# Dynamic time warping stage of a decoder kernel: low weight halves by TensorE and ScalarE, a wider backward scan, one comparison inside the forward waves, paths read back batch by batch

## The chip, the core and the metric

The kernel runs on one core of a Trainium2 chip. The metric is the device time of one execution in microseconds (us). A core has a matrix engine (TensorE, in the profile PE, its weight loads PEld), a vector engine (VectorE, DVE), a scalar engine (ScalarE, ACT), a general engine (GpSimd, POOL) and a queue engine (SyncE, SP) that here issues all transfers (DMA). The engines run on their own and wait for each other on semaphores.

## The reference, cut to what matters

Two decoder layers on x of shape (4, 1024, 256). The change lies in two neighbouring parts of the second layer:

```python
x = x + _L1_xattn_ref(ctx_1024, _layernorm(x))      # alignment by dynamic time warping
x = x + _L1_ffn_ref(_layernorm(x), sim, gates, q_proj, k_proj, v_proj, o_proj)   # 16 experts

def _align_one(small, large):           # small: 77 context rows, large: 1024 rows
    D = _pairwise_euclidean(small, large)
    R = _dtw_cost(D)                    # R[i,j] = D[i,j] + min(R[i-1,j], R[i,j-1], R[i-1,j-1])
    i_idx, j_idx, valid = _backtrack(R, T_small, T_large)   # from the corner: diagonal, up or left
    return zeros.at[j_idx].add(small[i_idx] * valid)        # a column of the path takes its rows

def _gating(h, sim, gates):
    logits = _l2norm(h, -1) @ _l2norm(sim, 0) - sigmoid(gates)      # then top choices and softmax
```

## The kernel before, in words

Four batches pass one after the other through the first layer, the cosine attention and the distances to the context rows, which are written to a padded tensor in memory. Then `finish_*` (lines 2314 to 2346) does, for all four batches together, the warping and then the experts. Only this end is touched.

**Forward waves.** The 1024 columns are cut into 16 lanes of `LW` = 64 columns. A batch takes 32 partitions, of which 16 hold its lanes, so the four batches lie side by side. Lane l works on context row w - l in wave w, so there are `WAVES` = 92 waves. A wave on DVE (`wave`, lines 1334 to 1347) is a minimum of two shifted views of the row before (L1342), a shuffle that brings the neighbour lane's last cell (L1344), and a scan along the 64 columns (L1346). ACT copies each row from a ring of four (`rows4`) into `costs` (`keep`, L1279) and, between rows, squares the expert weights for their scale. The distances come in three pieces of waves (`PIECES`): POOL fills a piece with a large number, then SP loads it (lines 1231 to 1236). POOL also sets the seeds, and the first wave waits for `seeds_set`.

**Between.** Four passes over 92 x 64 cells (L1374 to L1380) make 0/1 masks in 16 bits: whether the path came from above (`came_up`), whether from the diagonal (`came_diag`), and `left`, which is 1 - `came_up`.

**Backward waves.** Turns 0 to 91 walk back from the last wave (`wave_back`, lines 1391 to 1407): an addition of what moved down from the previous turn into `inject` (L1401), a shuffle (L1402), a scan in reversed order, cell = left x cell + inject (L1404), and a product of the step masks with the new row (L1407), which gives the next turn's two addends in `taken`. The first turns are written out, the rest is a loop of 22 turns of four waves each. ACT copies each row into `path_cells` (L1310), which may lag by no more than the ring of four rows.

**Weights in two halves.** Between groups of four rows ACT prepares the expert weights: 32 parts of 128 x 384 and 8 of 128 x 512. It scales a part in place (L1491, L1484) and rounds it to 16 bits, the high half (L1496, L1487). POOL subtracts the high half from the scaled part and writes the low half (`split_low_pool`, L1502, L1508). The halves overwrite parts that are done, so a part waits for an earlier one. TensorE does nothing in this stage.

**From the path to the experts.** SP stores the path in three pieces, waits for all, and loads all four batches' rows with one transfer (L1248), then `sim` and `gates` (L1565, L1566). ACT squares `sim`, TensorE sums it, POOL takes a power (L1580), and DVE scales `sim` before it copies the path rows. Then TensorE multiplies path and context rows (`align_pe`, L1631), DVE adds and normalizes, TensorE transposes, ACT copies the transposed rows (L275), squares the eight row tiles for the norm (`square_z`, L1789), and makes the high half of the transposed rows (L1793). DVE makes the low half, then the gate's choices (some 25 short instructions), and the expert products start.

Every engine executes its own instruction list in the written order. There is no planner; the order is that of the functions `dtw_*`, `split_*` and `experts_*`.

Of the kernel before, what the change touches and what calls it, by code (L numbers as in the profile page):

```python
# [15 lines left out]
F16 = mybir.dt.float16  # L16
# [69 lines left out]
def program(nc, t, out):  # L86

    ctx = ExitStack()
    with ctx:
# [1117 lines left out]
        left = r.take(WAVES, LW + 2, dt=BF16)  # L1207
# [4 lines left out]
        taken = zr.take(2, 2, LW + 1)  # L1212
        inject = zr.take(LW)
        path_padded = nc.dram_tensor("path", (B, PADDED, T), F32)
        skew_loaded = [sem(f"skew_loaded_{i}") for i in range(3)]
        dtw_done, path_in = sem("dtw_done"), sem("path_in")
# [14 lines left out]
        def dtw_sp(sp):  # L1231
            sp.wait_ge(pad_stored, 16 * 2 * B)
            for i, (w0, w1) in enumerate(PIECES):
# [14 lines left out]
            sp.dma_start(path_rows, path_padded.ap()[:, PAD:PAD + S2, :].rearrange("b i j -> i b j")).then_inc(path_in, 16)  # L1248

        def dtw_pool(g):  # L1250
# [11 lines left out]

            step(g.memset(rows4, BIG))
            step(g.memset(taken, 0.0))
            for b in range(B):
# [5 lines left out]
                step(g.memset(taken[32 * b:32 * b + 1, 1, 0, LW - 1:LW], 1.0))  # L1271
# [3 lines left out]
        def dtw_act(a):  # L1275
# [27 lines left out]
            with a.Fori(end + O_SUMS, WAVES // 4) as i:  # L1303
                for k in range(4):
                    keep(4 * i + k, k)
            a.wait_ge(w_root, 2)

            def keep_path(turn, k):
                a.wait_ge(path_row_ready, turn + 1)
                a.activation(path_cells[:, turn * -1 + (WAVES - 1), :], rows4[:, k, 0:LW], ACT.Copy).then_inc(path_kept, 1)  # L1310
# [3 lines left out]
            split_part(a, 0, True)  # L1314
            split_part(a, 1, True)
# [5 lines left out]
            for i in range(DC * E // 2, WAVES // 4):  # L1321
                for k in range(4):
                    keep_path(4 * i + k, k)
                for m in ((0, 1) if i == DC * E // 2 else (i - DC * E // 2 + 1,)):
                    split_o(a, m)

        def dtw_dve(v):
            own = Own(v, dtw_own)
            own(v.memset(costs[:, 0, :], BIG))
            v.wait_ge(seeds_set, 2 + 2 * B)  # L1330
# [3 lines left out]
            def wave(w, k, first):  # L1334
# [10 lines left out]
                own.wait()  # L1345
# [7 lines left out]
            def waves(first_turn, end):  # L1353
                with v.Fori(first_turn, end) as i:
                    own.enter(i - first_turn, 8)
# [14 lines left out]
            diag, above, beside = costs[:, 0:WAVES, 0:LW], costs[:, 0:WAVES, 1:], costs[:, 1:, 0:LW]  # L1370
            came_up, came_diag = step[:, :, 0, 0:LW], step[:, :, 1, 0:LW]
# [1236 lines left out]
```

## Time and profile before

| | before |
|---|---|
| median of three runs | 3520.44 us (3519.69 to 3520.49) |
| profiled execution, its own time | 3520.67 us |
| its span | 3519.0 us |
| busy over the span | PE 2756.7, DVE 2473.3, ACT 1352.1, POOL 649.7 us |
| mean granted TensorE clock | 0.872 of full speed |

The span runs from the first to the last recorded instruction. The warping begins 2381 us into it and the experts fill the rest from about 2684 us. A row of a timeline gives start, duration, engine, line of the kernel, operation, output and inputs, and in brackets the idle time before it with what ended that time. Stage rows give for each engine its busy time and its number of instructions, then the granted TensorE clock (1.00 is full speed).

### The profile page before, as it was taken

The page shows a single profiled execution, that of the slowest core. Times are in us where ns is not written, and L with a number is a line of the kernel's source. Part 1 is how long each engine was busy: PE and PEld are TensorE (multiplying, and loading weights), DVE is VectorE, ACT ScalarE, POOL GpSimd, SP SyncE. Part 2 cuts the span into 40 slices and gives each one's busy share as a digit, 9 for nine tenths or more (in the row PEclk, how much of TensorE's full clock was granted, in tenths as well). Part 3 has the DMA queues.
Part 4 walks back from the last instruction along what each step waited for, and adds up shares of the span by engine and source line. Part 5 has one row for each costly group of instructions (what it writes and reads, how often), then busy time and mean ns, then how long its engine had stood idle before and what let it go on. Part 6 is the DMA issues. An engine that isn't in the chain of part 4 may idle for free.

```text
span 3519.0 us, 37233 instructions
## 1 busy us (share of the span) xinstructions
PE 2756.7 (78%) x12144; PEld 1595.1 (45%) x12144; DVE 2473.3 (70%) x4930; ACT 1352.1 (38%) x2514; POOL 649.7 (18%) x457
## 2 busy tenths in 40 slices
PE   3225989996988997889997989980006999999998
PEld 2003854443764434665344854440004656556564
DVE  6995587986487996487996585016875677676766
ACT  2323316753325763324772316544341141221313
POOL 2443001341000331100333000000121040130404
PEclk9557789998899998789998799995557999999999
DMA  4001000101000001000101000105010000000000
GB/s 151 0 0 43 1 1 10 25 16 47 1 1 7 22 19 50 1 1 1 25 19 53 1 1 10 28 13 116 0 16 17 1 1 13 1 13 1 13 1 13
DMA packets 57593, 65.85 MB, mean 19 GB/s; under 512 B 27723, under 2 KB 46656, under 8 KB 56768
## 3 DMA queue, kind: packets, MB, share of 16 engines
q1 hardware_dynamic: 57408, 63.51, 6.7%
q8 instruction: 101, 1.65, 0.2%
q14 instruction: 84, 0.69, 0.1%
HBM read 45.22 MB, written 9.88 MB: 16 GB/s over the span
## 4 chain that ended last, share of the span: by engine, by line
PE 56%; DVE 28%; issue 5%; ACT 2%; POOL 2%; DMA 2%; DVEq 1%; SPq 0%; POOLq 0%; ACTq 0%
PE psum L1667 13%; DVE arena L542 6%; PE psum L383 6%; PE psum L931 3%; PE psum L786 3%; PE psum L1727 3%; DVE arena L537 3%; PE psum L766 3%; PE psum L1045 3%; PE psum L949 2%; PE psum L1087 2%; PE psum L777 2%; PE psum L269 2%; PE psum L373 2%; PE psum L374 2%
## 5 line engine op out<-in xcount | busy, mean ns | idle before, releaser
L1667 PE MATMUL psum<-weights,arena 128*128 128x384 f16 x3072 | 534.7, 329 | 6.1 <-DVE arena L2028 3.2
L383 PE MATMUL psum<-arena,weights 128*128 128x512 f32 (+1 forms) x1024 | 523.0, 593 | 5.0 <-ACT arena L458 5.0
L458 ACT ACTIVATE arena<-psum,minus_scale 128x512 f32<-128x512 f32 x512 | 350.7, 686 | 216.8 <-PE psum L383 215.0
L2031 DVE SCALAR_TENSOR_TENSOR arena<-psum,arena 128x384 f32<-128x384 f32 x480 | 295.8, 616 | 193.1 <-PE psum L1667 182.0
L1667 PEld LDWEIGHTS psum<-weights,arena 128*128 128x128 f16 x3072 | 304.2, 99 | 195.0 <-issue 11.6
L597 POOL TENSOR_TENSOR arena<-arena 128x1024 f32<-128x1024 f32 x128 | 274.0, 2140 | 600.7 <-DVE arena L542 600.1
L542 DVE TENSOR_TENSOR_SCAN arena<-weights,arena 128x1026 f32<-128x1026 f32 x128 | 293.9, 2296 | 19.5 <-ACT weights L451 3.8
L246 POOL TENSOR_SCALAR shifted<-mean_var 128x4 f32<-128x4 f32 x40 | 10.0, 250 | 1216.6 <-DVE mean_var L223 1216.1
L1907 POOL TENSOR_TENSOR arena<-arena 128x512 f32<-128x512 f32 x112 | 147.7, 1322 | 405.7 <-ACT arena L1848 395.3
L383 PEld LDWEIGHTS psum<-arena,weights 128*128 128x128 f32 (+1 forms) x1024 | 166.1, 163 | 98.8 <-ACT arena L458 12.1
L451 ACT ACTIVATE weights<-arena,weights 128x512 f32<-128x512 f32 x256 | 169.1, 712 | 102.8 <-DVE arena L542 102.8
L373 PE MATMUL psum<-arena 128*128 128x512 f16 x512 | 194.3, 379 | 4.7 <-DMA arena<-arena 4.7
L374 PE MATMUL psum<-arena 128*128 128x512 f16 x512 | 194.0, 379 | 0.0
L275 ACT ACTIVATE z_both<-psum 128x512 f32<-128x512 f32 x96 | 55.9, 596 | 321.2 <-PE psum L269 320.9
L1727 PE MATMUL psum<-weights,arena 128*128 128x512 f16 x768 | 172.5, 379 | 7.8 <-DVE x_all L2060 4.6
L269 PE MATMUL psum<-ident,z_both 128*128 128x128 f32 x384 | 74.4, 354 | 122.0 <-DVE z_both L260 102.2
L931 PE MATMUL psum<-weights,z_both 128*128 128x352 f32 x512 | 164.6, 476 | 6.2 <-DVE arena L1000 3.4
L550 DVE TENSOR_TENSOR arena<-arena,psum 128x1024 f32<-128x1024 f32 x128 | 156.4, 1222 | 4.4
L537 DVE TENSOR_TENSOR arena<-arena,psum 128x1024 f32<-128x1024 f32 x128 | 154.8, 1210 | 4.6 <-PE psum L356 3.6
L2060 DVE SCALAR_TENSOR_TENSOR x_all<-psum,arena,x_all 128x256 f32<-128x256 f32 x256 | 122.3, 483 | 50.0 <-PE psum L1727 44.9
L1592 PE MATMUL psum<-arena,ones 128*128 128x16 f32 x4 | 1.0, 372 | 198.8 <-ACT arena L1585 198.8
L766 PE MATMUL psum<-arena 128*128 128x308 f32 x256 | 124.8, 660 | 21.3 <-DVE arena L879 18.2
(316 smaller groups left out, 4979.1 us busy)
## 6 DMA issues: line engine op xcount, KB each, us to landing
arena<-arena SPq DMA_DIRECT2D x64, 128.0 KB, 2.3
arena<-head_inv SPq DMA_DIRECT2D x32, 256.0 KB, 3.4
weights<-in_qkv SPq DMA_DIRECT2D x2, 3072.0 KB, 17.1
weights<-gate_upT_kept SPq DMA_DIRECT2D x4, 1408.0 KB, 6.1
x_all<-in_x SPq DMA_DIRECT2D x4, 1024.0 KB, 12.1
weights<-in_cWkv SPq DMA_DIRECT2D x4, 1024.0 KB, 10.7
out<-x_all SPq DMA_DIRECT2D x4, 1024.0 KB, 4.4
weights<-downT_kept SPq DMA_DIRECT2D x4, 640.0 KB, 7.1
```

What stands on the lines that cost most here:

```text
L373: pe.matmul(psum[:, i % 3, :], keys, q_parts[:, hd, at], start=True, stop=False)
L374: pe.matmul(psum[:, i % 3, :], keys, q_swapped_parts[:, hd % 2, at], start=False, stop=True).then_inc(s2_psum, 1)
L383: pe.matmul(psum[0:rows, 3 + turn % 2, :], value_and_ones(kt, hd), expd[:, i % 2, :], start=kt == 0, stop=kt == NT - 1).then_inc(pv2_done, 1)
L458: a.activation(expd[:, i % 2, :], psum[:, i % 3, :], ACT.Exp, bias=minus_scale[:, :], scale=SCALE / QK ** 2).then_inc(exp_done, 1)
L537: v.tensor_tensor(to[:, :, 1:], u[:, :, at], both(5 + 2 * j % 3), ALU.mult).then_inc(w_done, 1)
L542: v.tensor_tensor_scan(flat, dA[:, j % RING].rearrange("p m x -> p (m x)"), flat, 0.0, ALU.mult, ALU.add).then_inc(scan_done, 1)
L597: g.tensor_tensor(y[:, :, at], y[:, :, at], h[:, j % RING, :, 1:], ALU.add).then_inc(y_added, 1)
L766: last = pe.matmul(psum[:, 2 * m + i, 0:SH], qT[:, m, k * P:(k + 1) * P], k_heads[:, m, 4 * i:4 * i + 4, :].rearrange("p h s -> p (h s)"), ...
L931: last = pe.matmul(psum[:, 2 * i + half, 0:FQ], zT[:, c, k * P:(k + 1) * P], wT[:, c, half * FQ:(half + 1) * FQ], start=c == 0, stop=c == ...
L1667: last = pe.matmul(psum[:, n % PROJ_BANKS, 0:W3], zT_parts[:, of_z, c, k * P:(k + 1) * P], w_parts[:, c, e, of_w, :], start=c == 0 and j == 0,
L1727: last = pe.matmul(psum[:, O_BANKS[u % 4], :], ao_parts[:, of_a, k * P:(k + 1) * P], o_parts[:, m, of_w, :], start=j == 0, stop=j == 2)
L2031: step_ = v.scalar_tensor_tensor(qkv[:, k, :], src, router_w[:, k, e:e + 1], qkv[:, k, :], ALU.mult, ALU.add)
```

## The change

1. POOL's subtraction of the halves is gone. ACT writes the high half from the unscaled part with the scale folded in. TensorE forms (scale x identity) x part minus identity x high half in a PSUM bank, and ACT copies the bank to the low half.
2. A backward turn has no addition. Row and addends are interleaved: `taken` holds two addends per cell, `left_and_one` holds `left` and a constant one, so a scan of 128 elements does cell = left x cell + a, then cell = 1 x cell + b. The rows are now 2 x 64 wide, the product reads and writes every second element. POOL writes the ones before it sets the seeds.
3. The comparison for `came_diag` is made per forward wave between shuffle and scan, and its pass between the sweeps is gone. `left` is made by ACT, and the last pass waits for it.
4. `sim` and `gates` are loaded ahead of the first distances, and their preparation runs during the sweeps. Path rows are loaded in four transfers, each waited for by its own batch.
5. `square_z` is gone; POOL gets the norm from the normalization's mean variance and rstd. Logits of the first batch are interleaved with its transposes.

```diff
-        left = r.take(WAVES, LW + 2, dt=BF16)
+        left_and_one = r.take(WAVES, LW + 1, 2, dt=BF16)
+        left = left_and_one[:, :, :, 0]
...
+        MOVED = 2 * LW + 4
+        taken = zr.take(2, MOVED)
+        back4 = zr.take(4, 2 * LW + 2)
+        def cells(row):
+            return row[:, 2 * LW::-2]
...
         def dtw_sp(sp):
             sp.wait_ge(pad_stored, 16 * 2 * B)
+            sp.dma_start(sim, by_chunk(t["sim"])).then_inc(small_in, 16)
+            sp.dma_start(gates_row, t["gates"].partition_broadcast(P)).then_inc(small_in, 16)
...
-            sp.dma_start(path_rows, path_padded.ap()[:, PAD:PAD + S2, :].rearrange("b i j -> i b j")).then_inc(path_in, 16)
+            for b in range(B):
+                sp.dma_start(path_rows[:, b, :], path_padded.ap()[b, PAD:PAD + S2, :]).then_inc(path_in[b], 16)
...
+            step(g.memset(left_and_one[:, :, :, 1], 1.0))
             step(g.memset(rows4, BIG))
...
+            a.wait_ge(up_made, 1)
+            a.activation(left[:, :, LW:0:-1], step[:, :, 0, 0:LW], ACT.Identity, bias=ones[:, 0:1],
+                         scale=-1.0).then_inc(left_made, 1)
             a.wait_ge(w_root, 2)
+            idents_act(a)
+            experts_setup_act(a)
...
             with a.Fori(1, DC * E // 2) as i:
                 for k in range(4):
                     keep_path(4 * i + k, k)
-                split_part(a, 2 * i, False)
-                split_part(a, 2 * i + 1, False)
+                split_high(a, 2 * i)
+                split_low(a, 2 * i - 1, 3)
+                split_high(a, 2 * i + 1)
+                split_low(a, 2 * i, 2)
...
-                own.wait()
+                both_ready = own.last
+                own(v.tensor_tensor(came_diag[:, w], before[:, 0:LW], before[:, 1:], ALU.is_le))
+                v.wait_ge(*both_ready)
                 v.tensor_tensor_scan(now[:, 1:], least, d_skew[:, w, :], now[:, 0:1], ALU.min,
                                      ALU.add).then_inc(row_ready, 1)
...
-            own(v.tensor_tensor(came_diag, diag, above, ALU.is_le))
             own.wait()
-            own(v.tensor_scalar(left[:, :, LW:0:-1], came_up, -1.0, 1.0, ALU.mult, ALU.add))
+            v.sem_inc(up_made, 1)
             own(v.tensor_tensor(came_diag, came_diag, came_up, ALU.mult))
             own.wait()
+            v.wait_ge(left_made, 1)
             own(v.tensor_tensor(came_up, came_up, came_diag, ALU.subtract))
...
-                own.wait_counted()
-                own(v.tensor_tensor(inject, down[:, 0, 0:LW], down[:, 1, 1:], ALU.add))
-                own(v.stream_shuffle(now[:, LW:LW + 1], before[:, 0:1], FROM_RIGHT))
-                own.wait()
-                v.tensor_tensor_scan(now[:, LW - 1::-1], left[:, w, 0:LW], inject[:, ::-1], now[:, LW:LW + 1],
-                                     ALU.mult, ALU.add).then_inc(path_row_ready, 1)
+                moved = taken[:, (k + 1) % 2, 2:2 + 2 * LW]
+                move_to = bass.AP(z_both, taken_at + k % 2 * MOVED + 2 * LW, [[NT * D + DC * T, P], [3, 2], [-2, LW + 1]])
+                own(v.stream_shuffle(now[:, 0:1], before[:, 2 * LW:2 * LW + 1], FROM_RIGHT))
+                own.wait()
+                if not first:
+                    v.wait_ge(path_kept, turn - 3)
+                v.tensor_tensor_scan(now[:, 1:2 * LW + 1], left_and_one[:, w, 0:LW, :].rearrange("p x s -> p (x s)"), moved,
+                                     now[:, 0:1], ALU.mult, ALU.add).then_inc(path_row_ready, 1)
                 v.wait_ge(path_row_ready, turn + 1)
-                own(v.tensor_tensor(taken[:, k % 2], step[:, w], now.unsqueeze(1).to_broadcast([P, 2, LW + 1]), ALU.mult))
+                own(v.tensor_tensor(move_to, step[:, w], cells(now).unsqueeze(1).to_broadcast([P, 2, LW + 1]), ALU.mult))
...
+        def split_high(a, i, first=False):
             if not first:
-                a.wait_ge(w_low, i - 1)
+                a.wait_ge(w_less, i - 1)
+            a.activation(part_of[:, bass.ds(i, 1), 0, :], whole_of[:, bass.ds(i, 1), :], ACT.Identity,
+                         scale=w_up).then_inc(w_high, 1)
+
+        def split_low(a, i, bank):
+            a.wait_ge(w_less, i + 1)
+            a.activation(part_of[:, bass.ds(i, 1), 1, :], psum[:, bank:bank + 1, 0:W3], ACT.Copy).then_inc(w_low, 1)
...
+        def less_high_pe(pe):
+            pe.wait_ge(w_diag, 3)
+            for i in range(DC * E + PAIRS):
+                bank = 2 + i % 2
+                pe.wait_ge(w_high, i + 1)
+                if i >= 2:
+                    pe.wait_ge(w_low, i - 1)
...
+                pe.matmul(to, scale_by, whole, start=True, stop=False)
+                pe.matmul(to, minus_ident, high, start=False, stop=True).then_inc(w_less, 1)
...
+            for g in range(NT // 2):
+                transpose_z(pe, 0, lambda k: pe.wait_ge(z_ready, k + 1), pairs=(g,), first_bank=3)
+                if g >= 1:
+                    logits_pe(pe, 0, FIRST, pairs=(g - 1,))
+            logits_pe(pe, 0, FIRST, pairs=(NT // 2 - 1,))
...
-            for k in range(NT):
-                square_z(a, 0, k)
...
         def finish_pe(pe):
             split_pe(pe)
             experts_setup_pe(pe)
+            less_high_pe(pe)
+            pe.wait_ge(w_low, DC * E + PAIRS)
             experts_start_pe(pe)
-            pe.wait_ge(w_low, DC * E + PAIRS)
```

## Rows read from the trace of the kernel before

**Rows 1.** Stages: busy time and instruction count by engine, TensorE clock, DMA share, GB/s.
```profile
2495.20:2645.50 150.30, 0.00 (x0) 0.00 (x0) 111.31 (x460) 63.62 (x171) 37.59 (x39) 0.50 0.08 9
2645.50:2693.00 47.50, 22.07 (x86) 16.48 (x86) 21.05 (x65) 12.75 (x29) 9.25 (x12) 0.57 0.11 30
```
**Rows 2.** Timeline at the start of the forward waves, POOL and DVE.
```profile
2383.94 1.38 POOL L1253 MEMSET arena<- 128x1536 f32 x1
2384.89 0.23 DVE L1342 TENSOR_TENSOR z_both<-z_both 128x64 f32<-128x64 f32 x1 [3.74 <-DMA arena<-distances]
```
**Rows 3.** Groups by line and shape: total busy us, mean ns; a POOL fill.
```profile
L2233 POOL MEMSET weights<- 96x4096 bf16 x1 | 3.5, 3507 | 0.1
```
**Rows 4.** Timeline of one forward wave inside the loop, DVE.
```profile
2436.11 0.15 DVE L1344 STREAM_SHUFFLE z_both<-z_both 128x1 f32<-128x1 f32 x1
2436.41 0.35 DVE L1346 TENSOR_TENSOR_SCAN z_both<-arena,z_both 128x64 f32 x1
```
**Rows 5.** Timeline of the passes between the sweeps, DVE.
```profile
2478.79 6.29 DVE L1375 TENSOR_TENSOR arena<-arena 128x5888 bf16<-128x5888 f32 x1
...
2486.72 3.32 DVE L1378 TENSOR_TENSOR arena<-arena 128x5888 bf16<-128x5888 bf16 x1
2490.08 3.32 DVE L1380 TENSOR_TENSOR arena<-arena 128x5888 bf16<-128x5888 bf16 x1
```
**Rows 6.** Groups by line and shape: ACT, two lengths of one kind of instruction.
```profile
L441 ACT ACTIVATE arena<-arena 128x1024 f32<-128x1024 f32 x8 | 8.0, 1048 | 0.0
L438 ACT ACTIVATE arena<-arena 128x2048 f32<-128x2048 f32 x4 | 7.6, 1911 | 0.0
```
**Rows 7.** Timeline of one backward loop turn, POOL and DVE, and the next turn's first product.
```profile
2508.01 0.91 POOL L1502 TENSOR_TENSOR weights<-weights 128x384 f16<-128x384 f32 x1 [5.04 <-ACT weights L1496]
2508.05 1.02 DVE L1407 TENSOR_TENSOR z_both<-arena,z_both 128x130 f32<-128x130 f32 x1 [0.15 <-DVE z_both L1404]
...
2509.17 0.93 POOL L1502 TENSOR_TENSOR weights<-weights 128x384 f16<-128x384 f32 x1 [0.25 <-ACT weights L1496]
...
2509.59 0.65 DVE L1404 TENSOR_TENSOR_SCAN z_both<-arena,z_both 128x64 f32<-128x64 f32 x1 [0.18 <-DVE z_both L1402]
...
2510.40 0.29 DVE L1407 TENSOR_TENSOR z_both<-arena,z_both 128x130 f32<-128x130 f32 x1 [0.15 <-DVE z_both L1404]
2510.73 0.23 DVE L1401 TENSOR_TENSOR z_both<-z_both 128x64 f32<-128x64 f32 x1
...
2510.88 0.15 DVE L1402 STREAM_SHUFFLE z_both<-z_both 128x1 f32<-128x1 f32 x1
2511.21 0.35 DVE L1404 TENSOR_TENSOR_SCAN z_both<-arena,z_both 128x64 f32<-128x64 f32 x1 [0.18 <-DVE z_both L1402]
...
2511.72 0.29 DVE L1407 TENSOR_TENSOR z_both<-arena,z_both 128x130 f32<-128x130 f32 x1 [0.15 <-DVE z_both L1404]
...
2514.62 1.03 DVE L1407 TENSOR_TENSOR z_both<-arena,z_both 128x130 f32<-128x130 f32 x1 [0.15 <-DVE z_both L1404]
```
**Rows 8.** Groups by line and shape: the long scans of the first layer.
```profile
L542 DVE TENSOR_TENSOR_SCAN arena<-weights,arena 128x1026 f32<-128x1026 f32 x128 | 293.9, 2296 | 19.5 <-ACT weights L451 3.8 <-DVE arena L537 1.5
```
**Rows 9.** Chain that ended last, in order of time: start, length, what.
```profile
2377.75 3.13 DMA distances<-arena
2649.40 7.81 DMA arena<-in_gates
2662.78 2.06 PE psum L1631 x4
```
**Rows 10.** Timeline from the path's load to the high halves.
```profile
2648.63 0.29 SPq L1248 DMA_DIRECT2D arena<-path  x1
...
2675.19 1.34 ACT L275 ACTIVATE z_both<-psum 128x512 f32<-128x512 f32 x2 [0.26 <-PE psum L269]
...
2676.58 4.78 PE L1639 MATMUL psum<-arena,z_both 128*128 128x16 f32 x32 [0.69 <-ACT z_both L275]
...
2680.62 1.99 ACT L1793 ACTIVATE arena<-z_both 128x1024 f16<-128x1024 f32 x2
```

More of the change, by code:

```diff
@@ L1368, in dtw_dve @@
             v.wait_ge(row_kept, WAVES)
-            diag, above, beside = costs[:, 0:WAVES, 0:LW], costs[:, 0:WAVES, 1:], costs[:, 1:, 0:LW]
-            came_up, came_diag = step[:, :, 0, 0:LW], step[:, :, 1, 0:LW]
+            beside = costs[:, 1:, 0:LW]
             own.wait()
@@ L1431, in program @@
         later = Region(arena)
-        causal = later.take(P)
         qkv = later.take(NT, 3 * HD)
@@ L1444, in program @@
         zT_parts = r.take(2, DC, T, dt=F16)
-        sim, sim_square = r.take(DC, E), r.take(DC, E)
-        gates_row, sim_norm, rank, minus_half16 = (r.take(E) for _ in range(4))
-        rank_int = r.take(E, dt=I32)
         (logit, gated, active, first1, weighed, first2, rest_logit, router, router_w) = (r.take(NT, E) for _ in range(9))
@@ L1452, in program @@
         router_next = r.take(NT, E)
-        z_square = r.take(D)
+        z_var = r.take(NT)
+        assert r.at <= beside_dtw
+        r = Region(arena, beside_dtw)
+        causal = r.take(P)
+        sim, sim_square = r.take(DC, E), r.take(DC, E)
+        gates_row, sim_norm, rank, minus_half16 = (r.take(E) for _ in range(4))
+        rank_int = r.take(E, dt=I32)
+        ident_up, ident_o_up, minus_ident = r.take(P), r.take(P), r.take(P, dt=F16)
         (w_squared, w_summed, w_total, w_root, w_scaled, w_high, w_low) = (
@@ L1588, in experts_setup_pe @@
         def experts_setup_pe(pe):
-            pe.wait_ge(weights2_in, 16 * 3)
+            pe.wait_ge(small_in, 16 * 2)
             pe.wait_ge(sim_sq_ready, 1)
             for c in range(DC):
-                last = pe.matmul(psum[:, 0, 0:E], ones[:, :], sim_square[:, c, :], start=c == 0, stop=c == DC - 1)
+                last = pe.matmul(psum[:, 4, 0:E], ones[:, :], sim_square[:, c, :], start=c == 0, stop=c == DC - 1)
             last.then_inc(sim_psum, 1)
@@ L1633, in align_pe, with logits_pe @@
             last.then_inc(aligned_psum, 1)
-        def logits_pe(pe, b, bank):
-            pe.wait_ge(zT_ready, 4 * (b + 1))
-            for k in range(NT):
-                for c in range(DC):
-                    last = pe.matmul(psum[:, bank, k * E:(k + 1) * E], zT[:, c, k * P:(k + 1) * P], sim[:, c, :],
-                                     start=c == 0, stop=c == DC - 1)
-            last.then_inc(l_psum, 1)
+        def logits_pe(pe, b, bank, pairs=range(NT // 2)):
+            for g in pairs:
+                pe.wait_ge(zT_ready, 4 * b + g + 1)
+                for k in (2 * g, 2 * g + 1):
+                    for c in range(DC):
+                        last = pe.matmul(psum[:, bank, k * E:(k + 1) * E], zT[:, c, k * P:(k + 1) * P], sim[:, c, :],
+                                         start=c == 0, stop=c == DC - 1)
+                if g == NT // 2 - 1:
+                    last.then_inc(l_psum, 1)
         def experts_start_pe(pe):
@@ L1800, in experts_start_act @@
             for g in range(NT // 2):
-                keep_zT_pair(a, 0, g, 4 + g)
-            for k in range(NT):
-                square_z(a, 0, k)
+                keep_zT_pair(a, 0, g, 3 + g)
             for c in range(DC):
```

118 lines of the change are left out of this document (52 added, 66 removed).

## The prediction, made before the changed kernel was run

> **What bounds the kernel now.** I read the page first, but its shares over the whole span say little here: TensorE is busy for 78% of it and yet does nothing in the two sweeps that the change rewrites. So the second view is that of the stages. In the backward sweep, 150.3 us long, TensorE executes no instruction, VectorE is busy for 111.3 us, ScalarE for 63.6 and GpSimd for 37.6 [rows 1]. No engine is full, so the sweep is a chain of short dependent steps, and I price it by the distance between starts, not by busy time. The third view is the chain that ended last, which puts the joint between warping and experts on transfers [rows 9]. The last is the timeline, for single waves.
>
> Two kinds of product stand in one loop turn [rows 7]. The clean one takes 0.29 us, the one that starts 0.04 us after a GpSimd subtraction takes 1.02, and ends when that subtraction has ended. A scan started under the second subtraction takes 0.65 instead of 0.35 us and ends with it too, while the addition and the shuffle near it keep their length where no subtraction covers them. So GpSimd's subtractions hold up VectorE's two-input instructions. That is 0.73 + 0.30 = 1.03 us of a turn of 6.57 us (2508.05 to 2514.62).
>
> **The change part by part.** Durations are from the profiled execution: 3520.67 us, of which the span is 3519.0, so 1.7 us lie around it and stay. It stands 0.2 us above the median of the three runs.
>
> *Ones before the seeds.* GpSimd fills 92 x 65 = 5980 elements of 16 bits at every second place before it sets the seeds. A fill of 4096 such elements, side by side, took 3.51 us [rows 3], 0.856 ns each, so 5.1 us. Queued behind it are the seeds, which the first wave waits for, the fill of the second piece, behind that SP's loads of that piece, and behind those the weights' loads. The seeds were done at 2383.94, when the next fill starts, and the first wave started at 2384.89, held by its transfer [rows 2]; now the seeds come at 2389.1. The first wave is 4.2 us late, and the second piece, whose fill began at 2383.94, is 5.1 late. I take **+5.1**; bounds +4.2 (only the first wave counts) and +10.2 (elements two apart cost double). The two small loads that SP now issues first lie under this fill; without that cover they would cost the first distances two issues, under 1 us at 0.29 us for a path issue [rows 10].
>
> *Comparison in the forward wave.* 92 instructions of 128x64 with two inputs; the nearest row is the backward addition, 0.23 us long, after which the next instruction starts 0.15 us later [rows 7]. It stands between shuffle and scan, and these start 0.30 us apart, of which the shuffle is 0.15 [rows 4]: the rest is the wait for the shuffle and the scan's address, in which the comparison fits if it can start as soon as the shuffle is under way. Bounds: 0 and 92 x 0.23 = 21 us. I take **+3**, 0.03 a wave, near the lower end because the gap is in the row.
>
> The Trainium skill, "VectorE: DVE Perf Modes", section Terms, says that a pipeline flush follows every instruction and that the next can't issue before the pipe is empty. By it the comparison would stand whole in the wave, +21 us in place of +3. The row above shows a shuffle that starts 0.08 us before the record of the addition ahead of it ends [rows 7], so starts do overlap here and the rule, taken literally, does not hold.
>
> *Between the sweeps.* The pass for `came_diag` and VectorE's pass for `left` go: the product that started at 2486.72 can follow the first pass at 2478.8, 7.9 us earlier [rows 5]. But the last pass must wait for ScalarE's `left`. ScalarE takes (1911 - 1048) / 1024 = 0.843 ns an element [rows 6], so 1048 + 4864 x 0.843 = 5.15 us for 5888, and some 0.3 for the two handovers, against 3.36 us from the product to the last pass (2486.72 to 2490.08): 2.1 us are given back. The clearing of the doubled rows, 260 more elements, adds about 0.3 by the 0.23 us that 64 elements take at most [rows 7]. Sum **-5.5**; bounds -7.9 (`left` hidden) and -0.4 (ScalarE at half its rate on elements two apart).
>
> *Backward sweep, subtractions gone.* 22 loop turns x 1.03 = **-22.6** [rows 7]. The later eight turns subtract once, on 128x512; I reckon them alike, since the stage's 39 GpSimd instructions are 37.6 us [rows 1] and the loop turns add up: 22 x 6.57 = 144.5 of 150.3. What takes GpSimd's place runs on engines with room: ScalarE's four instructions of 384 elements are 4 x 0.51 = 2.0 us by the slope above, where it had four already. TensorE's is new: by the path products at half clock, 2.06 us for four passes of 256 columns [rows 9], a pass of 384 takes 0.77. The two 32-bit passes and a third of at most that length are 2.3 us a part, 4.6 for two in a turn. The turn will be 5.1 us, so it fits, with 0.5 us in hand; the clock in this stage was 0.50 (1.2 GHz), the lower level, with no matmul before it [rows 1]. ScalarE takes the low half of the part before, not of the part just sent off, except at the turn's end, and the ring of four rows covers such a wait.
>
> *Backward sweep, wave.* Before [rows 7]: product to addition 0.33, to shuffle 0.15, to scan 0.33, to product 0.51, sum 1.32. Now: product to shuffle, no longer waiting, 0.22 (the 0.29 less the 0.08 by which the shuffle above starts ahead); to scan 0.33 plus 0.03 for the wait on the kept row, which moves here; to product 0.51 plus 64 more elements at (2296 - 351) / 962 = 2.02 ns [rows 8, 7], 0.13. Sum 1.22, so -0.10 a wave, 92 x 0.10 = **-9.2**. Bounds: -0.25 a wave (-23), if the added wait and the shuffle vanish behind the product; +0.11 (+10), if the product is not overtaken and costs double for elements two apart. No row shows VectorE at that spacing; I take the value nearest to the plain rows.
>
> *From path to experts.* The chain waited for `gates`, 7.81 us from 2649.40 to 2657.21, because it was queued behind 1.2 MB of path, and for the norms of `sim` made from it; the path products began at 2662.78 [rows 9]. All that now runs in the sweeps. What is late next is the first batch's path: issue at 2648.63 [rows 10], 308 KB, and the same 308 KB took 3.13 us on the way out [rows 9]. So 2651.8, plus 0.6 for copying half a batch: 2652.4, **-10.4**. TensorE also waits for the last low half; it is ready about 0.6 + 2.3 x 512 / 384 + 0.6 = 4.3 us after the last row, the path takes over 6. Bounds -11.5 and -5 (four loads share the engines and land together).
>
> *First gate.* ScalarE's eight squares stood between the last transposed copy, done at 2676.53, and the high halves at 2680.62 [rows 10]: 4.1 us. But TensorE now does two of four groups of logits ahead of the last transposes, 2 x 4.78 / 4 = 2.4 us. **-1.6**; bounds -4.1 and +0.7 (three groups in the way). The other batches' squares lay beside TensorE's products; I count nothing, and if they were in the way it is a gain.
>
> Sum: 5.1 + 3 - 5.5 - 22.6 - 9.2 - 10.4 - 1.6 = **-41.2 us**: 3479.5 for this execution, **3479** for the median.
>
> **The rivals.**
>
> *A. The comparison is not hidden.* Then each adds its distance of 0.15 us to the next start, 92 x 0.15 = 13.8 in place of 3: 3490. For it: in the loop, the wait follows the comparison, so the scan's address is worked out later. Against: the 0.30 us gap. The flush rule stands beside this case.
>
> *B. The wide scan costs what the addition saved.* The wave stays at 1.32 and only the stalls go: 3479 + 9 = 3488, and with a product at half rate 0.135 x 92 = 12 more, 3500. For it: twice the elements, and spacing that no row shows. Against: the 2.02 ns slope.
>
> *C. The wave shortens more.* Shuffle and waits vanish behind the product, -0.23 a wave: 3467. For it: the shuffle no longer depends on the product. Against: the scan still waits for it.
>
> *D. The stall isn't GpSimd's.* If it came from ScalarE's writing beside it, it stays: 3479 + 22.6 = 3502. Against: it ends with GpSimd's instruction both times [rows 7].
>
> *E. Slower: the round trip sets the pace.* High half on ScalarE, TensorE at half clock, low half on ScalarE. If ScalarE stands still for each round trip, a turn is 2 x (0.51 + 2.3 + 0.51) = 6.6 us plus four row copies at the stage's mean of 63.6 / 171 = 0.37 us, 8.1 in all against 6.57: 22 x 1.5 = +34, less the 9.4 us of the other parts, 3545. It decides from a turn of about 7.0 us. For it: every transfer between the engines is new, and 4.6 of 5.1 us is little room. Against: the order puts a part between sending and taking, and the clock can only rise.
>
> **How the numbers follow.** Forecast 0.50 (its own range 3470 to 3488), A 0.12, B 0.16, C 0.12, D 0.05, E 0.05. Range 3462 to 3500: it leaves out E and D (0.10), the far end of B (0.05) and the tail below C (0.04). What this kernel's measurement can't tell from no change is 0.2%, 7 us: all but E and mishaps that add up are below it. Faster 0.93, same 0.02, slower 0.05.
>
> **What would show it.** Right: products at L1407's place all near 0.3 us, a scan of 128 elements at 0.48, loop turns near 5.1 us, a forward wave near 0.86, the first wave near 2389, some 2 us of VectorE waiting for `left`, path products 7 us after the last row. Wrong: turns above 6 us with VectorE waiting for ScalarE's row copies (E), products of 1 us though GpSimd is idle (D), a forward wave near 1.0 (A), a strided product near 0.43 (B), path products held by the last low half.

## The result, and the profile after

The changed kernel took 3478.66 us (median of four runs, 3477.02 to 3479.86) against 3520.07 us of the kernel before on the same chip (3519.45 to 3520.49): a ratio of 0.9882, with a 95% interval of 0.9865 to 0.9899. The forecast was 3479. The profiled execution took 3479.86 us with a span of 3475.9, against 3520.67 and 3519.0.

The span is 43.1 us shorter, and every part of it can be located. Each part runs from the start of one instruction to the start of another that does the same step in both kernels (the first backward wave starts with its addition before, with its shuffle after):

| part | before, us | after, us | difference | forecast |
|---|---|---|---|---|
| up to GpSimd's first fill (not changed) | 2381.01 | 2379.99 | -1.0 | 0 |
| first fill to the first mask pass (ones, seeds, forward waves) | 91.64 | 96.08 | +4.4 | +8.1 |
| mask passes, up to the backward waves | 22.57 | 18.73 | -3.8 | -5.5 |
| backward sweep | 149.58 | 117.19 | -32.4 | -31.8 |
| last scan to path products | 17.98 | 8.00 | -10.0 | -10.4 |
| path products to the second round of expert products | 30.24 | 29.70 | -0.5 | -1.6 |
| the rest | 825.98 | 826.21 | +0.2 | 0 |

The parts add up to 43.1 us, where the forecast had 41.2. The time of that execution fell by 40.8, because 4.0 us of it lie outside the span, where the forecast left the 1.7 us of before; in the other three executions 1.8 to 2.4 us lie there.

The stages of the changed kernel, which answer to [rows 1]; the columns are the stretch, its length, the busy time and instruction count of TensorE, its weight loads, VectorE, ScalarE and GpSimd, the granted clock, DMA share and GB/s:

```profile
2493.70:2612.50 118.80, 64.30 (x117) 23.82 (x117) 81.65 (x373) 60.29 (x168) 2.90 (x1) 0.64 0.10 12
2612.50:2642.50 30.00, 21.62 (x73) 16.60 (x74) 14.69 (x43) 7.62 (x11) 4.88 (x8) 0.50 0.16 46
```

GpSimd's 39 instructions in the sweep have become one, TensorE's none have become 117, and VectorE is busy for 30 us less. The clock in the sweep is 0.64, above the lower level of 1.2 GHz (0.50) now that TensorE has matmuls there, but the stage behind it is back at 0.50.

The start, as the timeline of GpSimd and VectorE has it; answers to [rows 2, 3]:

```profile
2380.57 6.71 POOL L1276 MEMSET arena<- 128x5980 bf16 x1
...
2389.66 0.23 DVE L1370 TENSOR_TENSOR z_both<-z_both 128x64 f32<-128x64 f32 x1 [9.54 <-POOL z_both L1285]
2389.68 4.74 POOL L1266 MEMSET arena<- 128x1536 f32 x2
```

The first wave now waits for the seeds, no longer for its transfer, and the fill of the ones ahead of them is 6.71 us long where I had 5.1. A forward wave inside the loop, answering to [rows 4]:

```profile
2436.15 0.15 DVE L1372 STREAM_SHUFFLE z_both<-z_both 128x1 f32<-128x1 f32 x1
2436.22 0.22 DVE L1374 TENSOR_TENSOR arena<-z_both 128x64 f32 x1
2436.45 0.35 DVE L1376 TENSOR_TENSOR_SCAN z_both<-arena,z_both 128x64 f32 x1
2436.83 0.23 DVE L1370 TENSOR_TENSOR arena<-z_both 128x64 f32 x1
```

The comparison (L1374) starts 0.07 us after the shuffle, and the scan 0.30 us after it, as before. The passes between the sweeps, answering to [rows 5]:

```profile
2482.38 6.97 ACT L1321 ACTIVATE arena<-arena,ones 128x5888 bf16<-128x5888 bf16 x1 [6.48 <-DVEq L1405]
2482.44 3.33 DVE L1406 TENSOR_TENSOR arena<-arena 128x5888 bf16<-128x5888 bf16 x1 [0.15 <-DVE arena L1403]
...
2489.46 3.32 DVE L1409 TENSOR_TENSOR arena<-arena 128x5888 bf16<-128x5888 bf16 x1 [3.69 <-ACT arena L1321]
```

ScalarE's `left` takes 6.97 us, and VectorE's last pass stands 3.69 us for it. One turn of the backward loop, answering to [rows 7]; VectorE's scans and products, and what the other engines do beside them:

```profile
2535.49 0.49 DVE L1430 TENSOR_TENSOR_SCAN z_both<-arena,z_both 128x128 f32<-128x128 f32 x1 [0.29 <-DVE z_both L1426]
...
2535.59 1.65 PE L1551 MATMUL psum<-weights,arena 128*128 128x384 f32 x2 [1.63 <-ACT weights L1523]
2535.82 0.60 ACT L1523 ACTIVATE weights<-weights,w_scale  x1
2536.11 0.30 DVE L1433 TENSOR_TENSOR z_both<-arena,z_both 128x130 f32<-128x130 f32 x1
...
2536.33 0.15 DVE L1426 STREAM_SHUFFLE z_both<-z_both 128x1 f32<-128x1 f32 x1
...
2536.76 0.48 DVE L1430 TENSOR_TENSOR_SCAN z_both<-arena,z_both 128x128 f32<-128x128 f32 x1 [0.27 <-DVE z_both L1426]
2537.04 0.53 PE L1552 MATMUL psum<-weights,arena 128*128 128x384 f16 x1
...
2539.84 0.30 DVE L1433 TENSOR_TENSOR z_both<-arena,z_both 128x130 f32<-128x130 f32 x1
...
2540.22 0.01 DVE L1426 LOAD_MASK_SELECT z_both<-z_both  x1
...
2540.68 0.48 DVE L1430 TENSOR_TENSOR_SCAN z_both<-arena,z_both 128x128 f32<-128x128 f32 x1 [0.29 <-DVE z_both L1426]
```

Four scans start in 5.19 us (2535.49 to 2540.68), against a turn of 6.57. No product is longer than 0.30 us, the doubled scan is 0.48 to 0.49, and each scan stands idle for 0.27 to 0.29 us before it, which the trace puts down to the shuffle. That label will turn out not to explain it. The chain that ended last, behind the sweep, answers to [rows 9]:

```profile
2614.09 1.84 DMA path<-arena
2615.95 3.34 DMA arena<-path
2619.99 2.06 PE psum L1663 x4
...
2631.50 1.72 PE psum L1672 x8
...
2634.15 1.52 PE psum L1672 x8
```

The gates are gone from it; the first batch's path, 3.34 us, stands in their place.

### The profile page after: what moved, and what is told of

The parts are those of the page before. It is cut to its first block, busy times and chain, and to the rows that moved or that the text cites. A ratio compares the mean times of both kernels' runs of the same rounds, so it can differ in the third digit from the quotient of the medians.

```text
span 3475.9 us, 37333 instructions
## 1 busy us (share of the span) xinstructions
PE 2823.5 (81%) x12264; PEld 1619.9 (47%) x12264; DVE 2446.9 (70%) x4928; ACT 1342.4 (39%) x2454; POOL 618.4 (18%) x426
## 4 chain that ended last, share of the span: by engine, by line
PE 60%; DVE 25%; issue 5%; ACT 3%; POOL 3%; DMA 1%; DVEq 1%; SPq 0%; POOLq 0%; ACTq 0%
PE psum L1704 13%; PE psum L383 8%; DVE arena L542 5%; PE psum L931 4%; PE psum L786 3%; PE psum L766 3%; PE psum L1764 3%; PE psum L1045 3%; DVE arena L537 3%; PE psum L949 2%; PE psum L373 2%; PE psum L374 2%; PE psum L1087 2%; PE psum L777 2%; PE psum L269 2%
## 5 line engine op out<-in xcount | busy, mean ns | idle before, releaser
L356 PE MATMUL psum<-arena,weights 96*128 96x512 bf16 x128 | 55.9, 437 | 105.1 <-DVE arena L550 96.2
## 6 DMA issues: line engine op xcount, KB each, us to landing
weights<-in_cWkv SPq DMA_DIRECT2D x4, 1024.0 KB, 10.4
```

## The experiments

Each was timed beside the kernel before. "After" is the changed kernel, 3478.66 us; all but the last are edits of it. My theory was the ledger of the forecast: stalls under GpSimd gone, one instruction fewer in the wave, two transfers off the chain. The rivals are those named there.

**The subtractions back on GpSimd.** All else of the change stays.

```diff
-                split_high(a, 2 * i)
-                split_low(a, 2 * i - 1, 3)
+                split_part(a, 2 * i, False)
...
+            g.tensor_tensor(part_of[:, i, 1, :], whole_of[:, i, :], part_of[:, i, 0, :], ALU.subtract)
```

> The changed kernel with only the low halves given back to GpSimd (scale in place, round, subtract, as before). Theory: GpSimd's subtractions hold up VectorE's two-input instructions, about 1.03 us in each of 22 loop turns: the turn goes from 5.20 to about 6.2 us, products near 1 us come back, the time is 3479 + 22 = 3501 us. Rival D (the stall came from ScalarE's writing or something else beside it): turns stay at 5.2 us and the time within 3 us of 3479.

It took 3494.36 us, ratio 0.9928 (0.9912 to 0.9945). The timeline of its loop turn:

```profile
2535.01 0.60 ACT L1556 ACTIVATE weights<-weights,w_scale  x1
2535.09 0.30 DVE L1426 TENSOR_TENSOR z_both<-arena,z_both 128x130 f32<-128x130 f32 x1
2535.18 0.97 POOL L1567 TENSOR_TENSOR weights<-weights 128x384 f16<-128x384 f32 x1 [3.88 <-ACT weights L1561]
2535.74 0.70 DVE L1423 TENSOR_TENSOR_SCAN z_both<-arena,z_both 128x128 f32<-128x128 f32 x1 [0.27 <-DVE z_both L1419]
2536.34 0.91 POOL L1567 TENSOR_TENSOR weights<-weights 128x384 f16<-128x384 f32 x1 [0.18 <-ACT weights L1561]
2536.58 0.82 DVE L1426 TENSOR_TENSOR z_both<-arena,z_both 128x130 f32<-128x130 f32 x1
2537.75 0.48 DVE L1423 TENSOR_TENSOR_SCAN z_both<-arena,z_both 128x128 f32<-128x128 f32 x1 [0.27 <-DVE z_both L1419]
```

A scan under a subtraction is 0.70 us and a product 0.82, against 0.48 and 0.30 beside none: 0.74 us a turn, and the turn is 5.94. With the subtractions ScalarE's scaling in place came back too (L1556), and TensorE's products went. But the first two rows show that scaling over a product which keeps its 0.30 us, and both instructions that are stretched start inside a subtraction and end 0.15 to 0.29 us behind its end. So rival D falls. The Trainium skill ("SBUF — State Buffer", section "SBUF: two separate sides") says that VectorE and GpSimd share a pair of ports under an exclusive lock, which a VectorE instruction with two SBUF inputs takes against a GpSimd one that reads SBUF. These rows agree. The price was 15.7 us, not the 22.6 of the forecast. In the new wave the scan and the product start 0.56 and 0.24 us into the subtraction that holds them up, in the old one 0.42 and 0.04 [rows 7], so less of it is left to wait for: how much a stall costs depends on where in the wave it falls.

**The addition by itself.** The narrow scan and the addition come back, and ScalarE's `left` stands side by side again; the ones are still filled, to keep the start as it is.

```diff
-        left_and_one = r.take(WAVES, LW + 1, 2, dt=BF16)
+        left = r.take(WAVES, LW + 2, dt=BF16)
...
+                own(v.tensor_tensor(inject, down[:, 0, 0:LW], down[:, 1, 1:], ALU.add))
```

> The changed kernel with the backward wave of before: addition, shuffle, scan of 64, product side by side; GpSimd's fill of ones is kept as a fill of the same shape elsewhere. Theory: the wide wave saves what the loop turns show, (6.57 - 1.03 - 5.20) / 4 = 0.085 us a wave, so the turn is 5.54 us, the backward sweep 7.8 us longer, and since ScalarE now writes its left masks side by side, that pass takes 5.2 instead of 6.97 us and the last mask pass starts 1.7 us earlier: together 3485 us. Rival B (the wide scan costs what the addition saved): the turn stays at 5.2 us, 3477. If the mask pass stays at 6.97 us, its length is not from the spacing.

It took 3484.76 us, ratio 0.99 (0.9883 to 0.9916). From the first backward scan to the last it is 124.8 us against 117.0, so folding the addition is worth 7.8 us of sweep (forecast 9.2), and rival B falls. This sweep is also that of the kernel before without its subtractions; there it was 149.2, so in the old wave they cost 24.4 us (forecast 22.6). With the addition back, 1.6 us are gained between the sweeps:

```profile
2481.88 5.37 ACT L1320 ACTIVATE arena<-arena,ones 128x5888 bf16<-128x5888 bf16 x1 [6.49 <-DVEq L1404]
...
2487.36 3.32 DVE L1408 TENSOR_TENSOR arena<-arena 128x5888 bf16<-128x5888 bf16 x1 [2.09 <-ACT arena L1320]
```

The same instruction takes 5.37 us where its 16-bit results lie side by side and 6.97 where they lie two apart.

**The comparison as one pass.** The forward waves lose it, and it runs once over 5888 elements behind the sweep.

```diff
-                own(v.tensor_tensor(came_diag[:, w], before[:, 0:LW], before[:, 1:], ALU.is_le))
...
+            own(v.tensor_tensor(came_diag, costs[:, 0:WAVES, 0:LW], costs[:, 0:WAVES, 1:], ALU.is_le))
```

> The changed kernel with the diagonal comparison taken out of the forward waves and made by one pass between the sweeps, as before. Theory: in the wave it costs nothing, so a pass of 6.3 us is simply added: 3485 us, forward wave in the loop still 0.83 us. Rival A (0.15 us a wave): the waves get 13.8 us shorter and the time falls to 3471. In between, 0.03 a wave as forecast: 3482.

It took 3491.34 us, ratio 0.9918 (0.9902 to 0.9935), worse than every theory had it. The span grew by 13.9 us: 6.2 between the first mask pass and the product (the pass), 2.3 in the forward waves, which are longer without the comparison (first to last scan 87.5 against 85.2), and 5.4 in the backward sweep, which the edit does not touch. Its loop turn there is 5.45 us, and the timeline shows where:

```profile
2511.20 0.48 DVE L1429 TENSOR_TENSOR_SCAN z_both<-arena,z_both 128x128 f32<-128x128 f32 x1 [0.18 <-DVE z_both L1425]
2511.82 0.30 DVE L1432 TENSOR_TENSOR z_both<-arena,z_both 128x130 f32<-128x130 f32 x1
2512.47 0.01 DVE L1425 LOAD_MASK_SELECT z_both<-z_both  x1 [0.35 <-issue]
```

Behind the last product of a turn, at the branch, the shuffle's mask starts 0.65 us after the product; in the changed kernel it was 0.38. VectorE waits for no other engine there ("issue"). The body is the same; only its place differs, 35 instructions earlier in VectorE's program. So two runs on place alone, in which a clear ahead of the loop is cut in pieces, two in the changed kernel (shown), four in the one with the pass:

```diff
-            own(v.memset(back4, 0.0))
+            own(v.memset(back4[:, 0:2], 0.0))
+            own(v.memset(back4[:, 2:4], 0.0))
```

> The clear of the four rings' rows before the backward sweep is cut in two halves: the same work, and the backward loop stands one instruction further on VectorE. Without a comparison in the waves the loop's turn had lasted 5.45 us instead of 5.20, with 0.32 us of issue before the shuffle behind the branch. Theory of the place: where the loop lies in VectorE's instruction stream sets what its branch costs; if one instruction decides, the turn is 5.45 us and the time 3484 us; if the steps of place are coarser, 5.20 us and 3479 us. Rival, that the longer turn has to do with the data or the waits: 5.20 us and 3479 us.

> The kernel with the comparison as a pass of its own, and its clear of the four rows cut in four: the backward loop stands three instructions further, at the same place of 32 as with the comparison in the waves (35 instructions earlier). Theory of the place: the turn falls from 5.45 to 5.20 us, 22 times, and the time from 3491.3 to about 3486 us, which leaves +7 us for the pass itself. Rival, that the turn is longer because of the waits or the data that the pass leaves: 5.45 us and 3491.5 us.

One instruction later, the changed kernel stays as it was: 3477.41 us, turn 5.20. Three instructions later, the kernel with the pass falls from 3491.34 to 3487.68 us (ratio 0.9908, 0.9892 to 0.9925), and its turn to 5.20:

```profile
2536.92 0.48 DVE L1432 TENSOR_TENSOR_SCAN z_both<-arena,z_both 128x128 f32<-128x128 f32 x1 [0.18 <-DVE z_both L1428]
2537.55 0.30 DVE L1435 TENSOR_TENSOR z_both<-arena,z_both 128x130 f32<-128x130 f32 x1
2537.93 0.01 DVE L1428 LOAD_MASK_SELECT z_both<-z_both  x1
```

Product to mask is 0.38 us again, 0.27 less, and the sweep from first to last scan 117.0. So where a loop lies in the program can cost it 5 us here. Which property of the place counts, the four places tried don't tell. The comparison in the wave is worth the remaining 9.0 us: 6.2 for the pass, 2.2 in the forward waves, and 0.6 in small differences elsewhere. The 2.2 come for the most part from the second forward loop, whose turn is 3.84 us without the comparison and 3.64 with it; whether that comes from the comparison or from the place of that loop was not tested.

**The ones behind the fills.** GpSimd fills them as 32-bit words after the seeds and both pieces; ScalarE writes `left` over one half of each word later.

```diff
-            step(g.memset(left_and_one[:, :, :, 1], 1.0))
...
             fill_piece(2)
+            step(g.memset(ones_area, 1.0))
```

> The changed kernel with the ones filled behind the three pieces of distances, as one 32-bit fill over both halves (0 and 1.0 in one word), when GpSimd is idle. Theory: the fill of 6.7 us is on the path to the first wave and to the second piece; without it the first wave starts 5.8 us earlier and the time is 3473 us. Rival: the third piece, queued behind 3 MB of weights, ends the wait all the same; then 1 us or less is gained, 3478. The fill itself: 5.1 us if the 1.6 us over the estimate came from the spacing of 16-bit elements, 6.7 if it did not.

It took 3472.22 us, ratio 0.9863 (0.9847 to 0.988): 6.4 us less. The timeline shows the price of the spacing too:

```profile
2388.19 5.09 POOL L1289 MEMSET arena<- 128x5980 f32 x1
```

The same count of elements took 6.71 us as 16-bit ones two apart. The first wave waits 4.22 us for its transfer again.

**ScalarE's round trip in series.** It asks for each low half right after it has written the high half, instead of one part later.

```diff
                 split_high(a, 2 * i)
-                split_low(a, 2 * i - 1, 3)
-                split_high(a, 2 * i + 1)
                 split_low(a, 2 * i, 2)
+                split_high(a, 2 * i + 1)
+                split_low(a, 2 * i + 1, 3)
```

> ScalarE asks for the low half of a pair of rows right after it has written the high half, so that the way to TensorE and back stands in its own chain of work, and no longer beside the next high half. Theory of rival E: ScalarE's turn then sets the pace: four path rows of 0.26 us, two high halves of 0.6, twice TensorE's half-clock passes and the way to them of about 2.3 us, two low halves of 0.48, some 7.8 us in place of 5.20 in the turns that split, and VectorE waits for its kept rows: up to 16 x 2.6 = +40 us at the most, 3500 to 3518 us. Theory of the forecast, that the four rows of the ring and VectorE's own turn set the pace: only where ScalarE falls more than three rows behind does VectorE wait; at 7.8 us a turn it would, so a time of 3479 to 3485 us would mean that TensorE's part of the way is well below 1.5 us.

It took 3513.07 us, ratio 0.998 (0.997 to 0.999): 34 of the change's 41 us are gone. ScalarE's own timeline, and below it a row of VectorE's waits (us in total, times, longest):

```profile
2535.48 0.61 ACT L1523 ACTIVATE weights<-weights,w_scale  x1
2538.25 0.49 ACT L1528 ACTIVATE weights<-psum 128x384 f32 x1 [2.15 <-PE psum L1552]
2541.39 0.49 ACT L1528 ACTIVATE weights<-psum 128x384 f32 x1 [2.15 <-PE psum L1552]
2542.72 0.61 ACT L1523 ACTIVATE weights<-weights,w_scale  x1
...
DVE z_both L1430 <- ACT arena L1329: 35.8, 16, 2.3
```

It stands 2.15 us for each answer, its turn is 7.24 us (2535.48 to 2542.72), and VectorE waited 35.8 us in 16 waits for the kept rows. Rival E's mechanism is real, with about its price; the skewed order in the change is what keeps it off the chain.

**One load of the path.** One transfer for four batches in place of one for each.

```diff
-            for b in range(B):
-                sp.dma_start(path_rows[:, b, :], path_padded.ap()[b, PAD:PAD + S2, :]).then_inc(path_in[b], 16)
+            sp.dma_start(path_rows, path_padded.ap()[:, PAD:PAD + S2, :].rearrange("b i j -> i b j")).then_inc(path_in[0], 16)
```

> The path is loaded back by one transfer of all four batches in place of one for each. Theory of the forecast: the first batch's diagonal no longer lands 3.3 us after its issue but when the whole transfer does, 6.9 to 7.8 us as in the kernel before; nothing else stands between the last scan and the expert products, so about +4 us: 3482 to 3483 us, and the step from the last scan to the first path product 11.5 to 12.5 us instead of 8.0. Rival: the order of the path products alone gave the 10 us, and the transfer in four pieces nothing: 3479 us, the path's load 3.3 us or its wait covered.

It took 3483.11 us, ratio 0.9897 (0.988 to 0.9913). In its chain the load is 8.08 us instead of 3.34:

```profile
2615.48 8.08 DMA arena<-path
```

The path products start 12.7 us after the last scan instead of 8.0. That is about the +4.4 us, so the load by batch is part of the gain and not only the gates' earlier place.

**A better start and joint.** The late ones, and two moves: four clears ahead of the wait for `left`, two pairs of transposes ahead of the first logits.

```diff
             own(v.memset(back4, 0.0))
             own.wait()
+            v.wait_ge(left_made, 1)
+            own(v.tensor_tensor(came_up, came_up, came_diag, ALU.subtract))
```

> The ones of the wide scan are filled as 32-bit words after the seeds, the four clears of edges and rows stand before the wait for ScalarE's left mask, and two pairs of experts are transposed before the first logits. By the ledger: -6.4 us for the ones (measured by themselves), about -1.2 us for the clears, which ran after that wait (3.69 us of it, so that they fit), and 0 to -1 us for the transposes: 3470.5 to 3471.5 us. If the chain between the sweeps has another end than the left mask, the clears give nothing and it is 3472.

It took 3470.79 us, ratio 0.9865 (0.9848 to 0.9881); as reckoned.

**VectorE's loops written out.** On top of that version, first the backward loop, then both.

```diff
-            with v.Fori(1, WAVES // 4) as i:
-                own.enter(i - 1, 8)
-                for k in range(4):
-                    wave_back(4 * i + k, k, False)
-                own.leave(WAVES // 4 - 1)
+            for turn in range(4, WAVES):
+                wave_back(turn, turn % 4, False)
```

> The version with the late ones, the early clears and the two pairs of transposes, and VectorE's loop over the backward waves written out (88 waves in line, no branch, waits on constants). If a turn's branch and its registers cost what the last wave of a turn shows over the others (1.48 us against 1.18 and 1.27), a turn of four waves falls from 5.20 to between 4.7 and 5.1 us, 22 times: -2 to -10 us from 3470.8, so 3461 to 3469 us. Rival: instructions in line have to be loaded from memory and stall, and the time stays or rises by a few us; or ScalarE's kept rows set the pace, and 3470.8 stays.

> As the one before, and the forward loops of VectorE written out as well. A forward turn is 3.64 us and four inner waves of 0.83 are 3.32: 0.32 us over 18 to 20 turns, -5 to -7 us on top: 3455 to 3463 us. Rival: the longer first wave of each forward turn is a wait for ScalarE's kept rows, not for the branch; then it stays, and the time is that of the run before it.

They took 3437.87 us (ratio 0.9771, 0.9754 to 0.9787) and 3427.93 us (0.9739, 0.9723 to 0.9755): 33 and 43 us less than the version with loops, far more than the branches I had priced. A backward wave of the first:

```profile
2532.46 0.15 DVE L1429 STREAM_SHUFFLE z_both<-z_both 128x1 f32<-128x1 f32 x1
2532.65 0.48 DVE L1433 TENSOR_TENSOR_SCAN z_both<-arena,z_both 128x128 f32<-128x128 bf16 x1
2533.17 0.29 DVE L1436 TENSOR_TENSOR z_both<-arena,z_both 128x130 f32<-128x130 bf16 x1
2533.39 0.15 DVE L1429 STREAM_SHUFFLE z_both<-z_both 128x1 f32<-128x1 f32 x1
```

The scan starts 0.19 us after the shuffle instead of 0.43, the product 0.52 after the scan instead of 0.62: 0.93 us a wave where the loop had 1.18 to 1.48. The shuffle is the same, so the wait that the trace named after it in the loop, 22.1 us over the sweep (first row below), was not for the shuffle. The list of one line's instructions shows what stood there in the changed kernel, on VectorE's instruction queue (second row: count, shortest, median and longest in ns):

```profile
DVE z_both L1430 <- DVE z_both L1426: 22.1, 87, 0.3
...
L1430 DVEq FUSED_REGOPS  x88: 99/99/129, 2498.9 to 2611.8; - x88
```

In a loop the scan's address and the semaphore's target are worked out in registers, 88 times; where the loop is written out they are constants and the line is gone. Its 99 ns are less than half of the 0.24 us that the gap loses; what the rest of it is, no record shows, only that it goes with the loop. The trace of before had it in view: its forward waves start 0.83 us apart inside the loop and 0.72 to 0.73 in the waves written out ahead of it. In the second version VectorE stands 5.7 us for pieces of the distances, in the first 1.3: the faster waves reach a piece before it has landed, and a part of what they save is lost there.

**The kernel before, its loops written out.**

```diff
-            with v.Fori(1, WAVES // 4) as i:
...
+            for turn in range(4, WAVES):
+                wave_back(turn, turn % 4, False)
```

> The kernel before the change with VectorE's forward and backward loops written out, all else as it was. In the changed kernel the same step took 33 us in the backward sweep (1.27 to 0.93 us a wave) and 10 us in the forward one. Theory that the loop's registers cost each wave the same whatever stands in it: 41 to 45 us less here as well, 3475 to 3479 us, so that the change is still worth about 41 us in straight code (3428 plus the 8 us of the late ones, early clears and transposes is 3436 for the changed kernel written out). Rival, that the old backward wave hides part of it behind its stalls with GpSimd and its addition: 10 to 25 us less, 3495 to 3510 us, and the change is worth 60 us or more in straight code.

It took 3484.4 us, ratio 0.9901 (0.9883 to 0.9918): 35 us less, between the two theories and nearer to the first. Taken apart, the backward sweep goes with the rival: from first to last scan it is 22.8 us shorter, where the changed kernel's became 32.5 shorter; the forward one is 14.9 shorter (11.2). Its stalls stay, and the timeline of a turn shows them at about their old size, 0.47 us on this scan and 0.49 on the addition:

```profile
2542.93 0.82 DVE L1401 TENSOR_TENSOR_SCAN z_both<-arena,z_both 128x64 f32<-128x64 bf16 x1
2543.78 0.29 DVE L1404 TENSOR_TENSOR z_both<-arena,z_both 128x130 f32<-128x130 bf16 x1
2544.21 0.72 DVE L1398 TENSOR_TENSOR z_both<-z_both 128x64 f32<-128x64 f32 x1
```

Its backward sweep, first to last scan, is 126.5 us against 84.5 of the changed kernel's with its loops written out: 42 us, more than the 32 in loops. So the change's gain does not come from the loops; they hid part of it.

## Why the prediction was right

The total came out within 1 us, but that closeness is in part luck: four terms were off by about 1 to 4 us and mostly cancelled, the parts of the span add up to 1.9 us more than forecast, and the time outside the span, which the forecast left as it was, grew by about as much. What the forecast had right are the two large terms and their mechanisms.

*Backward sweep*: -31.8 forecast, -32.4 measured. The mechanisms are shown by the runs that put back the subtractions (D falls) and the addition (B falls). The two put back singly cost 15.3 and 7.8 us of sweep, 23.1 of the 32.4: in the old wave the stalls were longer than in the new one, so the parts don't add up. In the order of the forecast they do: 24.4 for the subtractions out of the old wave (22.6 forecast), then 7.8 for the addition (9.2). Inside the wave one step was off: I had the scan start 0.36 us after the shuffle, and in the loop it is 0.43.

*Path to experts*: -10.4 and -10.0, with the load at 3.34 us for the 3.13 that I took; one load would have taken 8.08.

*Ones before the seeds*: too small, 5.1 for a fill of 6.71 us, and 6.4 us of time once it was moved; the upper bound had the spacing in it, with the doubling too high. *Between the sweeps*: too large a gain, the same error on ScalarE, 6.97 for 5.15 us. Both came from rows with elements side by side.

*Comparison in the wave*: +3 was too high. Inner waves of the loop take 0.83 us with it as without it, and from the start of the first wave to the first mask pass it is 1.4 us less than before. Rival A falls. The comparison starts 0.07 us into a shuffle of 0.15; so the flush rule of the Trainium skill ("VectorE: DVE Perf Modes", section Terms), by which, taken literally, it would have cost 21 us, does not hold here. With the loops written out a wave is 0.73 us with it and 0.72 to 0.73 without. The turns of the two long forward loops differ between the two kernels, either way (3.63 us before and 3.77 after in the first, 3.84 and 3.64 in the second); why, was not settled.

*First gate*: -1.6 for -0.5. The two groups of logits ahead of the last transposes took 1.72 and 1.52 us, not a quarter of 4.78 each: the granted clock there was 0.50, and over the 4.78 us of before it had been 0.76 on average, which the forecast overlooked.

Rival C falls with the measured wave. Rival E had the wrong bound, not the wrong mechanism: it set in only when the answers were taken in series.

## What to carry to other kernels

Price a chain of short instructions by the distance between their starts, and ask of each gap whether it is a wait for data or register work of a loop: the same gap outside the loop, in the first or last waves, answers it before anything is built. A two-input VectorE instruction beside a long GpSimd subtraction, as here, is priced with the subtraction's end, and its price changes whenever the order around it does. When one engine sends work to another and takes it back, let another part lie between, or the round trip becomes the pace.

## What the runs showed of the hardware that I had not expected

- A loop on VectorE with waits against registers and addresses from them cost the backward sweep 0.25 to 0.55 us per wave of three instructions (1.18 to 1.48 for 0.93) and the inner forward waves 0.10 (0.83 for 0.73); writing both sweeps out took 43 us off the same arithmetic (3470.79 to 3427.93).
- The branch of the same loop body cost 0.27 us more a turn in one of four places of the program, 5.4 us in all. The Trainium skill ("Advanced Engine Details and Errata", section "Control Flow Timing") gives about 108 ns for a compare-and-branch; between the last product and the next mask the loop shows 0.16 us more than inside a turn (0.38 for 0.22) in the cheap places and 0.43 in the dear one, so its figure fits the first at best.
- 16-bit elements two apart cost more than side by side on two engines: 6.71 us on GpSimd for 5980 elements, where as many 32-bit words took 5.09 and 16-bit elements side by side 0.856 ns each [rows 3]; 6.97 for 5.37 on ScalarE (5888). VectorE's product that writes 32-bit elements two apart did not slow down (0.30 us as before).
- GpSimd's instruction at L1614, 2.90 us long though it has only 16 elements, did not hold up the scans and products that ran beside it (0.48 and 0.30 us):

```profile
2498.81 2.90 POOL L1614 TENSOR_TENSOR arena<-arena 128x16 f32<-128x16 f32 x1 [32.83 <-DVE arena L1438]
2499.06 0.48 DVE L1430 TENSOR_TENSOR_SCAN z_both<-arena,z_both 128x128 f32<-128x128 f32 x1 [0.32 <-DVE z_both L1426]
```
